# Two products with C of the recurrence's last two turns: added on GpSimd, then summed by TensorE once

## The reference, cut to what matters

```
state = decay * state + dt_t[..., None] * b_t[:, None, :] * u_t[..., None]
y_t = jnp.sum(state * c_t[:, None, :], axis=-1) + D_param * u_t      # 16 states n, 256 channels
...
h = jax.nn.silu(hg) * hu            # per expert, hg = x w_gate, hu = x w_up
ye = h w_down ; y = sum over experts of combine * ye
```

## Time and profile before

| what | value |
|---|---|
| median of 3 runs | 649.26 us |
| the profiled execution's own time | 650.56 us |
| its span, first to last instruction | 648.7 us |
| mean granted TensorE clock | 0.947 of full |
| busy: PE, DVE, POOL, ACT | 85%, 82%, 61%, 57% |
| chain that ended last, by engine | PE 48%, DVE 21%, ACT 11%, POOL 11%, issue 8% |

### The profile page before, as it was taken

One profiled execution on the slowest core, in us unless ns is written; L12 is line 12 of the kernel. 1 busy time (PEld: TensorE's weight loads), 2 busy tenths in 40 slices (PEclk: granted clock), 3 DMA queues, 4 the chain that ended last, 5 costly groups with the idle time before them and its releaser, 6 DMA issues.

```text
span 648.7 us, 6613 instructions
## 1 busy us (share of the span) xinstructions
PE 553.1 (85%) x1832; PEld 310.7 (48%) x1832; DVE 529.6 (82%) x729; ACT 370.0 (57%) x622; POOL 395.4 (61%) x345
## 2 busy tenths in 40 slices
PE   6698758899999968897869677858978999999997
PEld 3233222366769622333323233324434577788886
DVE  1879997746879678999999987989999967866674
ACT  4675333688214398867746544645655577655553
POOL 0035987652000201499999999987978657766664
PEclk9798987999799999899989987978999999999999
DMA  8000000800220001222212333322222443535340
GB/s 309 14 1 2 0 1 1 339 7 1 64 67 1 2 0 71 75 75 78 72 57 99 96 93 91 93 88 84 73 78 85 166 128 101 160 122 143 113 116 17
DMA packets 23796, 51.59 MB, mean 80 GB/s; under 512 B 2896, under 2 KB 3184, under 8 KB 23248
## 3 DMA queue, kind: packets, MB, share of 16 engines
q1 hardware_dynamic: 23760, 51.17, 24.7%
HBM read 49.83 MB, written 1.33 MB: 79 GB/s over the span
## 4 chain that ended last, share of the span: by engine, by line
PE 48%; DVE 21%; ACT 11%; POOL 11%; issue 8%; DMA 1%; DVEq 0%; POOLq 0%; SPq 0%
PE ps L1149 20%; POOL arena L2105 9%; DVE arena L2025 7%; PE ps L1084 5%; DVE arena L2000 4%; PE ps L753 3%; DVE arena L1752 3%; PE ps L1010 2%; PE ps L932 2%; DVE ps L1736 2%; PE ps L949 1%; ACT arena L1243 1%; PE ps L867 1%; ACT arena L1245 1%; PE ps L758 1%
## 5 line engine op out<-in xcount | busy, mean ns | idle before, releaser
L2105 POOL TENSOR_TENSOR arena<-arena 128x512 f32<-128x512 f32 x184 | 226.2, 1253 | 29.7 <-DVE arena L2025 24.2
L2025 DVE TENSOR_TENSOR_SCAN arena<-ps,carry,arena 128x512 f32<-128x512 f32 x128 | 156.4, 1263 | 0.0
L1563 ACT ACTIVATE ps<-arena,abase 128x512 f32<-128x512 f32 x128 | 88.4, 691 | 92.4 <-DVE arena L2025 92.2
L1084 PE MATMUL ps<-arena,core 128*128 128x512 f32 x256 | 130.0, 628 | 8.7 <-POOL arena L2105 8.1
L1149 PE MATMUL ps<-x_parts,w_hi 128*128 128x512 f32 x272 | 107.2, 423 | 20.3 <-POOL wD L2204 10.0
L2242 POOL TENSOR_TENSOR h_lo<-arena,h_hi 128x512 fp32r<-128x512 f32 x68 | 88.4, 1301 | 50.0 <-ACT h_hi L1613 49.4
L2000 DVE TENSOR_TENSOR arena<-ps,arena 128x1024 f32<-128x1024 f32 x64 | 76.8, 1201 | 11.4 <-PE ps L1189 11.4
L1084 PEld LDWEIGHTS ps<-arena,core 128*128 128x128 f32 x256 | 50.2, 201 | 57.1 <-issue 27.5
L1149 PEld LDWEIGHTS ps<-x_parts,w_hi 128*128 128x128 f32 x272 | 51.8, 190 | 45.2 <-POOL wD L2204 12.9
L2093 DVE TENSOR_TENSOR ps<-ps,arena 128x512 f32<-128x512 f32 x62 | 43.1, 696 | 32.5 <-PE ps L1149 24.9
L1149 PE MATMUL ps<-x_parts,wD 128*128 128x512 f32 x136 | 54.4, 400 | 0.0
(11 more groups left out here) (264 smaller groups left out, 1017.9 us busy)
## 6 DMA issues: line engine op xcount, KB each, us to landing
arena<-c_rows SPq DMA_DIRECT2D x64, 256.0 KB, 3.1
arena<-weight_rows SPq DMA_DIRECT2D x64, 256.0 KB, 3.2
arena<-in_wB SPq DMA_DIRECT2D x2, 2048.0 KB, 12.4
arena<-in_wD SPq DMA_DIRECT2D x8, 384.0 KB, 4.2
arena<-in_cstB SPq DMA_DIRECT2D x1, 1368.0 KB, 5.7
wC<-in_wC SPq DMA_DIRECT2D x1, 1056.0 KB, 12.0
x<-in_x SPq DMA_DIRECT2D x4, 256.0 KB, 4.6
arena<-slot_rows SPq DMA_DIRECT2D x4, 256.0 KB, 3.8
```

The source lines that it names most:

```text
L1084: mm(bank(c + 2 * (i % 2)), CORE_("eye"), PRC[:, (2 * q + c) % PR_RING, :], start=False, stop=(n == NS - 1)).then_inc(*done(f"y{n}_{c}", i))
L1563: A(bank(6 + c), ch(DTG[:, c, :], i), ACT.Exp, scale=ABASE[:, c * NS + n:c * NS + n + 1]).then_inc(*done(f"dec{n}_{c}", i))
L2025: nc.vector.tensor_tensor_scan(ST[:, k % ST_RING, :], bank(6 + c), DBU[:, (2 * q + c) % DBU_RING, :], CARRY[:, k:k + 1], ALU.mult, ALU.add ...
L2105: mul = lambda o, a, b: nc.gpsimd.tensor_tensor(o, a, b, ALU.mult)
```

## The change

Before the first expert turn GpSimd adds, for each half c, the product with C of turn 62 to that of turn 63, in place in the ring PRC (two new instructions, `pair_0` and `pair_1`). TensorE then sums the pair in one `y_sum`: `y_sum(62)` is gone, and `y_sum(63)` waits for the pair and stands in turn m = 3 behind the up product of that turn, where it was in turn m = 2. All else is as before.

```diff
@@ sequences() @@
-        elif LAG <= q < NQ + LAG - 1:
-            pe += y_names(q + (m > 0))
+        elif LAG <= q < NQ or m == LAG - 1:
+            pe += y_names(q)
...
-            pool.append((f"h_lo{e}", mi))
+            pool += (one("pair_0", "pair_1") if m == 0 else []) + [(f"h_lo{e}", mi)]
@@ y_sum(q) on TensorE @@
-                    pe.wait_ge(*upto(f"sc{n}_{c}", i))
+                    pe.wait_ge(*(upto(f"pair_{c}") if q == NQ - 1 else upto(f"sc{n}_{c}", i)))
@@ the expert turns on TensorE @@
-                if m < LAG - 1:
-                    y_sum(NQ + m + 1 - LAG)
+                if m == LAG - 1:
+                    y_sum(NQ - 1)
@@ GpSimd, between the 64 turns and the expert turns @@
+            for c in range(DI):
+                pool.wait_ge(*upto(f"sc{NS - 1}_{c}", LAST))
+                pair = [PRC[:, (2 * q + c) % PR_RING, :] for q in (NQ - 1, NQ - 2)]
+                nc.gpsimd.tensor_tensor(pair[0], pair[0], pair[1], ALU.add).then_inc(*done(f"pair_{c}"))
```

## The result

The changed kernel takes 652.51 us (median of 9 runs, 651.54 to 656.13) against 649.32 us for the kernel before (median of 9, 648.34 to 651.5). The ratio is 1.0057, 95% interval [1.0041, 1.0073], which is +3.7 us [+2.7, +4.7], a small slowdown that is clear of no change. By the two medians it is +3.2. The forecast was +3.8 us, 653.1.

What follows compares the result with a forecast made beforehand. TensorE was taken to bound the kernel from 509.55 us, a start set by VectorE. 0 + 1.72 - 0.1 + 0 + 2.2 = +3.8 us gave 653.1 us; the forecast's own range was 651.0 to 654.6, the whole range 650.8 to 654.9.

Steps and rivals of the forecast that it cites:

- What bounds the seam: VectorE's `hw` of turn 1 sets the up product of turn 3 at 509.55 us; TensorE bounds from there on.
- The sum that goes: Removing `y_sum(62)` at 504.10 us frees 1.72 us of TensorE that only becomes idle time; gain 0.
- The sum that moves: `y_sum(63)` goes from idle time to behind the up product of turn 3, delaying all later TensorE work: +1.72 us.
- -0.1 taken back: TensorE's wait for VectorE at 516.07 us gives back 0.1 us of the delay; bounds 0 and -0.4.
- GpSimd: Its two additions, 1.25 us each, end near 507.45 us, before TensorE wants the pair at 510.25; cost 0.
- The clock: The emptied gap before the up product of turn 3 likely drops TensorE's clock to 0.50: +2.2 us, bounds 0 and 3.1.
- The clock holds: Rival: TensorE's clock stays up over the gap, only the moved sum counts: +1.6 us, 650.9 us; chance 0.12.
- Less TensorE work is faster: Rival: 1.72 us fewer matmuls end the TensorE-bound tail from 509.55 us that much earlier: 647.5 us; chance 0.02.
- Absorbed later: Rival: later waits for VectorE, such as 0.73 us at 537.39, shrink and absorb delay: about 649.9 us; chance 0.04.
- GpSimd is late: Rival: additions take over 2 us each and `h_lo` becomes the wait: up to +0.3 us on the forecast; chance 0.02.
- Signs of being wrong: Clock stays 1.00 over the seam, up product of turn 3 starts before 508, or the 0.73 us wait at 537 goes.
- rival 2: Less TensorE work is a faster kernel, the tail from 509.55 us ending 1.72 us earlier: 647.5 us; chance 0.02.

Runs made afterwards that it cites:

- e1: Changed kernel with the pair's sum put back into turn 2, ahead of the up product of turn 3; 650.75 us, ratio 1.0009 [0.9994, 1.0023].
- e4: Changed kernel plus 18 filler matmuls in the gap, their result overwritten; 652.31 us, ratio 1.0036 [1.0022, 1.0050].
- c1: Changed kernel with the pair summed in turn 2 and gate products of turns 4 and 6 brought forward into the gap; 649.17 us, ratio 0.9995.
- c3: Kernel before, no pair, gate product of turn 4 ahead of the up product of turn 3, `gated` in turn 6; 649.03 us, ratio 1.0000.
- e3: Kernel before without the sum of turn 62 and with 16 of 512 columns of that of turn 63; 651.25 us, ratio 1.0024 [1.0012, 1.0037].
- e2: Kernel before with only `y_sum(63)` moved from turn 2 to turn 3, no pair; 652.01 us, ratio 1.0043 [1.0026, 1.0059].
- a1: Changed kernel, unedited, profiled in a second execution; 652.33 us (one), 139.27 us from the up product of turn 3 to the last matmul.
- c2: As c1, with VectorE's two `gated` instructions one turn later, in turn 6; 649.09 us, ratio 0.9986 [0.9970, 1.0001] against the kernel before.

## Why the prediction was right

- **What bounds the seam.** Right. VectorE's `hw` of turn 1 released the up product of turn 3 in every run, changed or not. In the kernel before, the changed one and e1 to e4 the chain is then TensorE's; in c1 to c3, where TensorE has less to do there, it goes over VectorE once more.
- **The sum that goes: 0.** Right, since the wait for VectorE ended where it did. What its absence uncovers is the clock's term: e3 removes both sums and is slower.
- **The sum that moves: +1.72, -0.1 taken back.** Right in size: 1.66 in e4. Its small part is less sure: the wait ahead of the up product of turn 5 is not gone but 0.08 us in e4 (517.74 + 0.23 to 518.05) where it was 0.11.
- **GpSimd: 0.** Right: 2.52 us for the two, no wait for the pair, and e1 is equal to before.
- **The clock: +2.2, bounds 0 and 3.1.** The fall came in both executions of the changed kernel and in e2 and e3. The price was 2.91 and 2.34 in the changed kernel, 1.26 in e3 and, less the 1.66, 2.89 in e2. So the 2.2, a mean of five stretches of another stage, was under both of the changed kernel's. By ratio +3.7 [+2.7, +4.7] less 1.66 leaves 2.0 [1.0, 3.1] for it. The rule behind the price held: all four are half of TensorE's busy time in the low stretch within 0.2 us. How much work would fall into that stretch was not foreseen, so that +3.8 met +3.7 within 0.1 is in part luck.
- **Rivals.** "The clock holds" fell with the trace. "Less TensorE work is faster" is refuted by e3. "Absorbed later" is refuted by the wait of 0.73 us ahead of the up product at 537, which stands in all traces with the same 0.73 (the changed kernel's is below): it hangs on TensorE. "GpSimd is late" by e1.
- **Signs of being wrong.** One of the three that the prediction names came true by the letter: the up product of turn 3 started before 508, at 507.71 and at 507.17 in a1. It was meant to catch rival 2, a start soon after that of turn 2. I put it badly, in absolute time: the whole seam is earlier, and from `hw` of turn 0 to `hw` of turn 1 it is 4.08 us before and after.
- **What was off.** The forecast's own range, 651.0 to 654.6, does not follow from its bounds: 649.26 + 1.6 is 650.9, and 3.1 more is 654.0. And I took -0.1 as the end of VectorE's part; c1 shows how near a second bound is. Behind the gap VectorE is so full that TensorE could not be made earlier there (c1: 0.00) without thinning VectorE too (c2: 1.05). That did not matter for a change that makes TensorE late.

```profile
540.10 0.50 PE L1149 MATMUL ps<-x_parts,w_hi 128*128 128x512 f32 x1 [0.73 <-DVE arena L2098]
```

What stays open is at which emptiness of the gap the clock falls: e1 with 3.08 us busy in 5.3 kept it in the profiled execution, e2 with 2.49 didn't, each seen once. Nor is it known in how many of the timed executions it fell. e1's lie at 648.5 to 649.0 and at 650.6 to 651.1, but those of the kernel before lie anywhere from 648.0 to 651.5, so they don't tell.

## What to carry to other kernels

Before work is taken off an engine or moved on it, ask which wait ends last at that place: matmuls that run while TensorE waits for another engine cost nothing here, and the same matmuls behind the wait cost nearly their full length. A sum put one turn later cost 1.66 us for 1.72 us of matmuls. A gap in TensorE's work that is made wider can also have a price after it: here the clock fell to 0.50 and the dense work behind ran at half speed, for 1.3 to 2.9 us lost. Filling the gap, even with products that nobody reads, took that price away in the trace (e4). Filling it with work that was due anyway pays only as far as the engine that feeds it has room.

## What the runs showed of the hardware

The clock fell over a gap that was not idle throughout: 1.21 us and 3.11 us idle with three matmuls between, 1.08 us busy in 5.4. It fell in different places, from 1.93 us before to 0.49 us before the work resumed, and stayed at half for 3.4 or 6.8 us; the same kernel paid 2.9 us in one execution and 2.3 in another, with 6.8 us at half in both. And less arithmetic was slower: 3.4 us of matmuls left out made the program 0.24% longer.
